# Moving every TensorE operand to a multiple of 128 bytes in an attention and token-mixing layer

## The chip, the cores and the metric

The kernel runs on one core of one Trainium2 chip. The time is the device time of one execution in microseconds, from start to end of the program. Three runs gave 1501.23, 1501.57 and 1502.23 us, median 1501.57 us. The profile is of one more execution.

## The reference

Eight sequences of 1024 tokens with 256 features. Each is normalised over its features, goes through attention with 8 query heads that share one key and one value head of 128 dimensions, and through a gated mix with the token before. Both results are added to the input.

```python
xn = layernorm(x)                                # x: 8 x 1024 x 256, float32
q = xn @ Wq + bq;  k, v = split(xn @ Wkv + bkv)  # q: 8 heads of 128; one k, one v
q, k = q + pe, k + pe                            # sinusoidal positions
p = softmax(causal(q @ k.T / sqrt(128)))         # per head, 1024 x 1024
attn = concat_heads(p @ v) @ Wo
xr, xk = mix of xn and xn one token earlier, with mu_r, mu_k
ffn = sigmoid(xr @ W_r.T) * (relu(xk @ W_k.T) ** 2 @ W_v.T)
out = x + attn + ffn
```

## The kernel before, in words

The precision is kept with pairs. Each operand of a product is split into a high part and a rest (`xt[0]`, `xt[1]`; `wq[0]`, `wq[1]`; and so on), and `product` (L1034) issues three matmuls for each: high by high, high by rest, rest by high. All are of type float32r. In `nc.tensor.matmul(out, a, m)` the first operand `a` is the standing one, loaded into the array by a weight load of 128 columns; `m` is the moving one, which streams past it. The transposes (`pT`, `xn`, `kv`) are of type float32, with the data standing and `ident` moving.

The queries are handled in 64 steps for each sequence (`turns`, L119). A step covers 16 tokens of all 8 heads. `turn` on TensorE (L1131) issues in a fixed order, written out by hand: the transposes of the probabilities of an earlier step (L1143), what the tables `TURNS` and `WO_AT` list for the step (`fill`, L1073: queries Q, keys and values KV, the gated mix FK, FR, FV, the output projection WO), the products of probabilities and values for each second step (L1181, L1190), and the scores of the step (L1211 through L1040). Which operand stands and which moves:

| product | standing | moving | columns |
|---|---|---|---|
| Q, KV, FK | `wq`, `wkv`, `wk` | `xt`, `xt`, `mh` | 256 |
| FR | `mh` | `wr` | 256 |
| FV | `kh` | `wv` | 256 |
| WO | `ot` | `wo` | 256 |
| probabilities by values | `v`, `vn`, `vs` | `pt` | 256 |
| scores | `qt` | `kt` | 16 to 512 |

Scores wider than 512 columns are made in two halves of equal width; the second half starts in `kt` wherever the first ends, a multiple of 32 bytes. VectorE adds the mask to the scores and writes `X` (L1019), ScalarE takes the exponential (L764), GpSimd divides by the sum (L571), and TensorE transposes, or VectorE does (L923) and DMAs carry `Y` to memory and back into `pt` (park L436, fetch L448).

The arrays of on-chip memory are laid out one after the other in the order in which `build` names them (L208 to L250), each rounded up to 32 bytes. The first, `xt`, starts at byte 640 of each partition. As every size up to `wo` is a multiple of 1024, `xt`, `mh`, `wv`, `kt`, `pt` and `wo` all start 128 bytes past a multiple of 256. Behind `wo` stands `gap`, an array of 64 bytes that nothing uses. So `wq`, `wk`, `wkv`, `wr`, `kh`, `qt`, `v`, `vs`, `vn` and `ot` start 192 bytes past a multiple of 256. Small tables then shift what follows: `ident` and `kv` start at 192, `xn` and `X` at 160, `Y` at 224, each past a multiple of 256. Slices that the program takes out of the standing arrays start 512 bytes apart or a multiple of that, and the slices of `pt` 128 bytes apart.

Of the kernel before, what the change touches and what calls it, by code (L numbers as in the profile page):

```python
# [5 lines left out]
H, D = 8, 128  # L6
P = 128
CT = E // P
CHUNK = 256
TPC = CHUNK // P  # L10
NC = T // CHUNK
NT = T // P
# [177 lines left out]
def build(nc, x_d, wq_d, wkv_d, wo_d, wr_d, wk_d, wv_d, bq_d, bkv_d, mu_d, pet_d, out_d, park_d):  # L190
# [6 lines left out]
    with ExitStack() as ctx:  # L197
        def sb(name, shape, dt=F):
            return ctx.enter_context(nc.sbuf_tensor(name, shape, dt))
# [4 lines left out]
        def sem(name):  # L204
# [6 lines left out]
        kt = [sb(f"kt{i}", [P, T], R) for i in range(2)]  # L211
        pt = [sb(f"pt{i}", [P, 2 + i, 2 * NT * P], R) for i in range(2)]
        wo = [sb(f"wo{i}", [P, H, E], R) for i in range(2)]
        gap = sb("gap", [P, 16])
        wq = [sb(f"wq{i}", [P, CT, H * D], R) for i in range(2)]
        wk = [sb(f"wk{i}", [P, CT, E], R) for i in range(2)]
        wkv = [sb(f"wkv{i}", [P, CT, 2 * D], R) for i in range(2)]
# [4 lines left out]
        vs = sb("vs", [P, TPC, D], R)  # L222
        vn = sb("vn", [P, NT, D], R)
        ot = [sb(f"ot{i}", [P, H, P], R) for i in range(2)]
        bq = sb("bq", [P, H])
        mu = sb("mu", [P, 4])
        omu = sb("omu", [P, 4])
        bkv = sb("bkv", [P, 2])
        pet = sb("pet", [P, T])
        mask = sb("mask", [P, WIDE], mybir.dt.bfloat16)  # L230
        gap2 = sb("gap2", [P, 24])
        ident = sb("ident", [P, P])
        xtok = sb("xtok", [P, NC, TPC, E])
        kv = sb("kv", [P, 2, CHUNK])
        stats = sb("stats", [P, TPC, 6])
        mv = sb("mv", [P, TPC, 2])
        rstd = sb("rstd", [P, TPC])
        vare = sb("vare", [P, TPC])
        half = sb("half", [P, TPC])
        xnt = sb("xnt", [P, CT, CHUNK + 1])  # L240
        qtmp = sb("qtmp", [P, QTMP, 2, CHUNK])
        mix = sb("mix", [P, CT, CHUNK])
        ka = sb("ka", [P, CT, CHUNK])
        gate = sb("gate", [P, TPC, E])
        xn = sb("xn", [P, TPC, E])
        X = sb("X", [P, 10, T // 2])
        bias = sb("bias", [P, 10])
        total = sb("total", [P, 10])
        rec = sb("rec", [P, 10])
        Y = sb("Y", [P, 2, 4, NT, 32])  # L250
        steps_of = X[:, 9, 0:P].rearrange("p (h c) -> p h c", h=H)

        pS = [pb(f"pS{i}", [P, 2, 512]) for i in range(2)]
# [82 lines left out]

        STAGE = {"wq0": X[:, 0:CT, :],
                 "wq1": X[:, CT:2 * CT, :],
                 "wkv": X[:, 4, :].rearrange("p (t n) -> p t n", t=CT),
                 "wk": X[:, 5, :].rearrange("p (t n) -> p t n", t=CT),  # L340
                 "wr": X[:, 6:6 + CT, E:2 * E],
                 "wv": X[:, 8:8 + CT, E:2 * E],
                 "wo0": Y[:, 0, :, :, :].rearrange("p a k c -> p a (k c)"),
                 "wo1": Y[:, 1, :, :, :].rearrange("p a k c -> p a (k c)")}
        W = {"wq0": [w[:, :, 0:H * D // 2] for w in wq], "wq1": [w[:, :, H * D // 2:H * D] for w in wq],
# [12 lines left out]
        def x_row(s, lo, hi):  # L358

            j, n = halves_of(s)  # L360
            return X[:, j:j + n, :].rearrange("p h n -> p (h n)")[:, lo:hi]
# [40 lines left out]
        def _(sp):  # L402
# [27 lines left out]
            def park(b, s):  # L430
# [3 lines left out]
                if k >= 4:  # L434
                    sp.wait_ge(landed[k % 4], 64 * (k // 4))
                sp.dma_start(park_d[k % 4, :, :, 0:nk * 32],  # L436
                             Y[:, k % 2, :, 0:nk, :].rearrange("p a k c -> p a (k c)")).then_inc(parked[k % 2], 16)

# [349 lines left out]
        def _(dve):  # L788
# [119 lines left out]
            def turn(b, it):  # L908
# [6 lines left out]
                if s in TURNED:  # L915
# [5 lines left out]
                    if k >= 2:  # L921
                        dve.wait_ge(parked[k % 2], 16 * (k // 2))
                    nc.vector.transpose(Y[:, k % 2, :, 0:nk, :].rearrange("p a k c -> p k a c"),  # L923
                                        x_row(s, 0, nk * P).rearrange("p (k a c) -> p k a c", a=4, c=32)
# [362 lines left out]
```

## Time and profile before

| | us |
|---|---|
| median of three runs | 1501.57 |
| the profiled execution, its own time | 1506.69 |
| its span, first to last instruction | 1504.9 |
| TensorE matmuls busy | 1482.6 |
| weight loads busy (beside the matmuls) | 1448.2 |
| VectorE busy | 1268.4 |
| GpSimd busy | 1128.9 |
| ScalarE busy | 1068.0 |

The mean granted TensorE clock was 0.997 of the full 2.4 GHz. Busy time is the union of what an engine's instructions cover. A matmul's recorded duration runs from its start until its last result, and the next matmul starts long before that, so durations of neighbours overlap; a run of equal matmuls is timed by the distance of the starts of the groups before and after it.

### The profile page before, as it was taken

What the parts mean: (1) busy time and instruction counts of PE and PEld (TensorE: products, weight loads), DVE (VectorE), ACT (ScalarE), POOL (GpSimd) and SP (SyncE); (2) the same over time, 40 slices, a digit from 0 to 9 for tenths busy, and PEclk for the clock granted to TensorE, in tenths of its full rate; (3) what the DMA queues carried; (4) which work ended last, traced back from release to release, by engine and by line L of the source; (5) the groups of instructions that cost most, each with busy time, mean ns of one, the idle gap of its engine ahead of it and who ended that gap; (6) DMA issues with size and microseconds to landing.
All of it is one profiled execution on the core that took longest, in us unless ns stands there. A gap on an engine that the chain in (4) does not pass through costs nothing.

```text
span 1504.9 us, 36254 instructions
## 1 busy us (share of the span) xinstructions
PE 1482.6 (99%) x11724; PEld 1448.2 (96%) x11724; DVE 1268.4 (84%) x3424; ACT 1068.0 (71%) x2563; POOL 1128.9 (75%) x1541
## 2 busy tenths in 40 slices
PE   7999999999999999999999999999999999999998
PEld 7999999999999999999999999999999999999998
DVE  6999878898788987998879888798977888789885
ACT  6777667776677767767677776776767777677764
POOL 6687777777777877777777776777777787777875
PEclk8999999999999999999999999999999999999999
DMA  4144422444224442244423444134441344403453
GB/s 129 48 131 129 142 75 64 134 125 147 72 65 133 135 134 68 83 120 137 134 60 88 127 128 144 46 98 128 134 141 34 113 131 138 136 27 108 119 157 105
DMA packets 225801, 164.39 MB, mean 109 GB/s; under 512 B 51792, under 2 KB 220880, under 8 KB 225616
## 3 DMA queue, kind: packets, MB, share of 16 engines
q1 hardware_dynamic: 224768, 161.69, 35.6%
q8 instruction: 96, 1.57, 0.4%
q14 instruction: 89, 0.73, 0.2%
q10 hardware_dynamic: 848, 0.40, 0.1%
HBM read 81.27 MB, written 77.59 MB: 106 GB/s over the span
## 4 chain that ended last, share of the span: by engine, by line
PE 81%; DVE 10%; issue 4%; POOL 3%; DMA 1%; ACT 1%; SPq 0%; DVEq 0%; POOLq 0%; ACTq 0%
PE pS L1040 27%; PE pO L1181 22%; PE pG L1040 13%; PE pG L1127 9%; PE pT L1143 8%; DVE X L1019 2%; DVE pt L943 1%; DVE Y L923 1%; DVE kt L831 1%; POOL X L571 1%; DVE xn L808 1%; DMA park_dram<-Y 1%; DVE mix L860 1%; POOL qt L527 1%; DVE qtmp L849 1%
## 5 line engine op out<-in xcount | busy, mean ns | idle before, releaser
L764 ACT ACTIVATE X<-X,bias 128x16 f32<-128x16 f32 (+56 forms) x512 | 376.1, 734 | 150.7 <-DVE bias L1019 149.0
L1040 PE MATMUL pS<-kt,qt 128*128 128x288 f32 (+41 forms) x2304 | 460.1, 329 | 4.5 <-DVE bias L1019 3.4
L571 POOL TENSOR_SCALAR X<-X,rec 128x16 f32<-128x16 f32 (+56 forms) x512 | 378.2, 739 | 44.2 <-DVE rec L913 33.4
L1040 PEld LDWEIGHTS pS<-kt,qt 128*128 128x128 f32 x2304 | 365.7, 189 | 17.1 <-issue 5.3
L546 POOL TENSOR_TENSOR pt<-pt 128x256 fp32r<-128x256 f32 (+5 forms) x192 | 316.6, 1649 | 60.3 <-ACT pt L686 59.8
L1181 PE MATMUL pO<-pt,v 128*128 128x256 f32 x2192 | 307.6, 284 | 1.2 <-DVE ot L998 0.9
L1019 DVE CUSTOM_DVE_ANT_1 X<-pS,mask 128x528 f32<-128x528 f32 (+31 forms) x256 | 245.6, 959 | 47.1 <-PE pS L1040 42.3
L1181 PEld LDWEIGHTS pO<-pt,v 128*128 128x128 f32 x2192 | 271.9, 189 | 2.6 <-DVE ot L998 2.1
L943 DVE TENSOR_TENSOR pt<-pt,pT 128x512 fp32r<-128x512 f32 (+3 forms) x440 | 207.6, 493 | 35.1 <-ACT pt L692 32.2
L757 ACT CAST ot<-pO 128x256 fp32r<-128x256 f32 x256 | 95.5, 373 | 184.0 <-PE pO L1181 117.8
L692 ACT CAST pt<-pT 128x512 fp32r<-128x512 f32 (+3 forms) x448 | 188.0, 450 | 30.8 <-PE pT L1143 30.5
L527 POOL TENSOR_TENSOR qt<-qtmp,qt 128x512 fp32r<-128x512 f32 x124 | 162.1, 1310 | 57.5 <-ACT qt L659 57.2
L1127 PE MATMUL pG<-wo,ot 128*128 128x256 f32 x1536 | 194.0, 283 | 2.2 <-ACT ka L739 1.5
L1143 PE MATMUL pT<-ident,X 128*128 128x128 f32 x1248 | 190.3, 274 | 0.9 <-DVE pt L943 0.6
L1127 PEld LDWEIGHTS pG<-wo,ot 128*128 128x128 f32 x1536 | 183.0, 189 | 3.5 <-ACT ka L739 2.8
L923 DVE STREAM_TRANSPOSE Y<-X 128x384 f32<-128x384 f32 (+5 forms) x192 | 172.5, 898 | 10.5 <-POOL X L571 9.4
L1181 PE MATMUL pO<-pt,vn 128*128 128x256 f32 x1096 | 171.1, 281 | 0.0
L686 ACT ACTIVATE pt<-pt 128x384 fp32r<-128x384 f32 (+5 forms) x192 | 150.2, 783 | 19.3 <-DMA pt<-park_dram 17.5
L1143 PEld LDWEIGHTS pT<-ident,X 128*128 128x128 f32 x1248 | 150.6, 141 | 10.4 <-issue 0.8
L998 DVE TENSOR_TENSOR ot<-pO,ot 128x256 fp32r<-128x256 f32 x256 | 107.1, 418 | 51.1 <-ACT ot L757 47.9
L1181 PEld LDWEIGHTS pO<-pt,vn 128*128 128x128 f32 x1096 | 146.6, 188 | 0.0
L569 POOL MEMSET X<- 128x16 f32 (+5 forms) x336 | 47.9, 142 | 130.6 <-DVE rec L913 129.7
(120 smaller groups left out, 2298.6 us busy)
## 6 DMA issues: line engine op xcount, KB each, us to landing
park_dram<-Y SPq DMA_DIRECT2D x32, 512.0 KB, 2.6
pt<-park_dram SPq DMA_DIRECT2D x128, 128.0 KB, 2.8
park_dram<-Y SPq DMA_DIRECT2D x32, 448.0 KB, 3.0
pt<-park_dram SPq DMA_DIRECT2D x128, 112.0 KB, 2.5
park_dram<-Y SPq DMA_DIRECT2D x32, 384.0 KB, 2.9
pt<-park_dram SPq DMA_DIRECT2D x128, 96.0 KB, 2.3
park_dram<-Y SPq DMA_DIRECT2D x32, 320.0 KB, 2.7
pt<-park_dram SPq DMA_DIRECT2D x128, 80.0 KB, 2.1
```

What stands on the lines that cost most here:

```text
L527: nc.gpsimd.tensor_tensor(qt[1][:, slot, :, 2 * p:2 * p + 2, :].rearrange("p t i q -> p i t q"), qtmp[:, p % QTMP, :, :].rearrange("p i (t ...
L546: nc.gpsimd.tensor_tensor(low, low.bitcast(F), high.bitcast(F), ALU.add).then_inc(turned_lo, 1)
L571: nc.gpsimd.tensor_scalar(x_row(s, 0, w), x_row(s, 0, w), rec[:, j:j + 1], sign(s), ALU.mult, ALU.mult).then_inc(normed, 1)
L692: nc.scalar.copy(pt_of(0, b, s)[:, s % 2, :, k:k + nk, :].rearrange("p a k c -> p k a c"), pT[u % 2][:, 0:nk * P].rearrange("p (k a c) -> ...
L764: nc.scalar.activation(x_row(s, 0, w), x_row(s, 0, w), ACT.Exp, bias=bias[:, j:j + 1], scale=-1.0, accum_out=total[:, j:j + 1]).then_inc(e ...
L923: nc.vector.transpose(Y[:, k % 2, :, 0:nk, :].rearrange("p a k c -> p k a c"), x_row(s, 0, nk * P).rearrange("p (k a c) -> p k a c", a=4, ...
L943: last = nc.vector.tensor_tensor(low[:, k:k + whole, :, :], high[:, k:k + whole, :, :].bitcast(F), pT[u % 2][:, 0:whole * P].rearrange("p ...
L1019: nc.vector.tensor_tensor_reduce(out=o, in0=scores, in1=m, scale=SCALE, scalar=HUGE, op0=ALU.add, op1=ALU.min, accum_out=bias[:, j:j + 1]) ...
L1040: last = nc.tensor.matmul(out, a[i], m[j], start=start and k == 0, stop=stop and k == n - 1)
L1127: last = nc.tensor.matmul(out[:, 0:E], ot[i][:, h, :], wo[j][:, h, :], start=(i, j, h) == (0, 0, 0), stop=i == 1 and h == H - 1)
L1143: last = nc.tensor.transpose(pT[u % 2][:, i * P:(i + 1) * P], x_row(s, (k + i) * P, (k + i + 1) * P), ident[:, :])
L1181: last = nc.tensor.matmul(summed, (vn if j else v[i])[:, k, :], pt_of(j, b, part)[:, :, :, k, :], start=n == 0, stop=n == 3 * nk - 1)
```

## The change

Nothing but the order of the arrays changes. `gap` goes, so that the ten arrays behind it move down by 64 bytes and start, like the six before them, 128 bytes past a multiple of 256. The small tables (`bq`, `mu`, `omu`, `bkv`, `stats` and the like) and `xnt` move to the end, behind the large arrays, and `Y` moves ahead of `xnt`. With them gone, `pet`, `mask`, `ident`, `xtok`, `kv`, `qtmp`, `mix`, `ka`, `gate`, `xn`, `X` and `Y` start at a multiple of 128; `ident`, `kv`, `xn`, `X` and `Y` at a multiple of 256. No instruction, wait or DMA is added, removed or moved.

```diff
         wo = [sb(f"wo{i}", [P, H, E], R) for i in range(2)]
-        gap = sb("gap", [P, 16])
         wq = [sb(f"wq{i}", [P, CT, H * D], R) for i in range(2)]
...
         ot = [sb(f"ot{i}", [P, H, P], R) for i in range(2)]
-        bq = sb("bq", [P, H])
-        mu = sb("mu", [P, 4])
-        omu = sb("omu", [P, 4])
-        bkv = sb("bkv", [P, 2])
         pet = sb("pet", [P, T])
...
         kv = sb("kv", [P, 2, CHUNK])
-        stats = sb("stats", [P, TPC, 6])
...
-        xnt = sb("xnt", [P, CT, CHUNK + 1])
         qtmp = sb("qtmp", [P, QTMP, 2, CHUNK])
...
         X = sb("X", [P, 10, T // 2])
+        Y = sb("Y", [P, 2, 4, NT, 32])
+        xnt = sb("xnt", [P, CT, CHUNK + 1])
+        bq = sb("bq", [P, H])
+        mu = sb("mu", [P, 4])
...
         bias = sb("bias", [P, 10])
         total = sb("total", [P, 10])
         rec = sb("rec", [P, 10])
-        Y = sb("Y", [P, 2, 4, NT, 32])
```

## Rows read from the trace of the kernel before

**Rows 1.** The page's busy times: engine, us, share of the span, instructions

```profile
PE 1482.6 (99%) x11724; PEld 1448.2 (96%) x11724; DVE 1268.4 (84%) x3424; ACT 1068.0 (71%) x2563; POOL 1128.9 (75%) x1541
```

**Rows 2.** Busy time by stretch, all engines; columns named in its first line

```profile
core 0: us, PE busy (x) PEld busy (x) DVE busy (x) ACT busy (x) POOL busy (x), PEclk, DMA share, GB/s
0.00:50.00 50.00, 40.32 (x281) 38.24 (x282) 38.18 (x123) 31.70 (x85) 31.51 (x58) 0.90 0.30 98
150.00:700.00 550.00, 545.45 (x4342) 533.55 (x4341) 468.14 (x1264) 393.16 (x949) 415.62 (x567) 1.00 0.36 108
700.00:1400.00 700.00, 697.16 (x5556) 681.99 (x5555) 593.13 (x1623) 503.52 (x1220) 533.41 (x731) 1.00 0.36 107
1460.00:1505.00 45.00, 40.56 (x310) 38.06 (x309) 26.30 (x51) 22.35 (x40) 24.73 (x23) 1.00 0.33 110
```

**Rows 3.** The page's chain that ended last, shares by engine

```profile
PE 81%; DVE 10%; issue 4%; POOL 3%; DMA 1%; ACT 1%; SPq 0%; DVEq 0%; POOLq 0%; ACTq 0%
```

**Rows 4.** Views of single tiles, matmuls: count, duration ns min/median/max, first and last start

```profile
L1040 PE MATMUL pS<-wv,kh x192: 276/276/367, 45.3 to 1374.6; 128*128 128x256 f32 x192
L1040 PE MATMUL pS<-wr,mh x192: 277/279/363, 34.0 to 1351.9; 128*128 128x256 f32 x192
L1040 PE MATMUL pG<-wr,mh x192: 277/279/363, 104.0 to 1462.9; 128*128 128x256 f32 x192
L1040 PE MATMUL pS<-mh,wk x192: 276/281/365, 20.2 to 1343.6; 128*128 128x256 f32 x192
L1040 PE MATMUL pG<-mh,wk x192: 276/276/386, 84.6 to 1428.5; 128*128 128x256 f32 x192
L1040 PE MATMUL pG<-xt,wq x924: 276/281/550, 15.4 to 1419.7; 128*128 128x256 f32 x185
L1040 PE MATMUL pS<-xt,wq x600: 276/276/561, 12.4 to 1370.3; 128*128 128x256 f32 x150
L1127 PE MATMUL pG<-wo,ot x1536: 276/281/391, 51.3 to 1501.9; 128*128 128x256 f32 x192
L1181 PE MATMUL pO<-pt,v x2192: 276/279/388, 35.8 to 1497.3; 128*128 128x256 f32 x200
L1181 PE MATMUL pO<-pt,vn x1096: 276/281/286, 36.2 to 1498.3; 128*128 128x256 f32 x183
```

**Rows 5.** Timeline of TensorE: start us, us, engine, line, operation, count

```profile
674.87 1.30 PE L1181 MATMUL pO<-pt,v 128*128 128x256 f32 x10
676.00 0.74 PE L1181 MATMUL pO<-pt,vn 128*128 128x256 f32 x5
676.58 1.12 PE L1040 MATMUL pS<-kt,qt 128*128 128x352 f32 x6
677.54 1.57 PE L1040 MATMUL pG<-xt,wq 128*128 128x256 f32 x12
...
681.91 1.34 PE L1181 MATMUL pO<-pt,v 128*128 128x256 f32 x10
683.09 0.75 PE L1181 MATMUL pO<-pt,vn 128*128 128x256 f32 x5
```

**Rows 6.** Groups by line and form, 730.21 to 730.23 us, the end of an FR

```profile
L1040 PE MATMUL pG<-wr,mh 128*128 128x256 f32 x3 | 0.5, 278 | 0.0
```

**Rows 7.** Groups by line, 725.95 us (first half) and 726.65 us (second)

```profile
L1040 PE MATMUL pS<-kt,qt 128*128 128x464 f32 x2 | 0.6, 372 | 0.0
L1040 PE MATMUL pS<-kt,qt 128*128 128x464 f32 x2 | 0.6, 374 | 0.0
```

**Rows 8.** Views of the tiles `kv` and `X`, transposes on TensorE

```profile
L1095 PE MATMUL pG<-ident,kv x46: 270/270/271, 80.1 to 1422.7; 128*128 128x128 f32 x46
L1143 PE MATMUL pT<-ident,X x1248: 270/272/457, 31.3 to 1491.2; 128*128 128x128 f32 x179
```

**Rows 9.** From the page's costliest groups and its DMA issues

```profile
L1019 DVE CUSTOM_DVE_ANT_1 X<-pS,mask 128x528 f32<-128x528 f32 (+31 forms) x256 | 245.6, 959 | 47.1 <-PE pS L1040 42.3
park_dram<-Y SPq DMA_DIRECT2D x32, 512.0 KB, 2.6
```

**Rows 10.** Waits, longest in total: engine, line, releaser, us, times, longest

```profile
ACT pt L686 <- DMA pt<-park_dram: 17.5, 25, 2.0
```

More of the change, by code:

```diff
@@ L234, in build @@
         kv = sb("kv", [P, 2, CHUNK])
-        stats = sb("stats", [P, TPC, 6])
[L236 to L239, printed above, removed]
-        xnt = sb("xnt", [P, CT, CHUNK + 1])
         qtmp = sb("qtmp", [P, QTMP, 2, CHUNK])
@@ L246, in build @@
         X = sb("X", [P, 10, T // 2])
+        Y = sb("Y", [P, 2, 4, NT, 32])
+        xnt = sb("xnt", [P, CT, CHUNK + 1])
+        bq = sb("bq", [P, H])
+        mu = sb("mu", [P, 4])
+        omu = sb("omu", [P, 4])
+        bkv = sb("bkv", [P, 2])
+        stats = sb("stats", [P, TPC, 6])
+        mv = sb("mv", [P, TPC, 2])
+        rstd = sb("rstd", [P, TPC])
+        vare = sb("vare", [P, TPC])
+        half = sb("half", [P, TPC])
         bias = sb("bias", [P, 10])
```

## The prediction

> **What bounds the kernel now.** I read the busy times first. TensorE's matmuls cover 99% of the span and the weight loads beside them 96%, VectorE 84% [rows 1]. Busy time overstates a pipelined engine, so the next view is the same by stretch: from 150 to 1400 us TensorE stands idle for 4.6 of 550 us and 2.8 of 700 us, and only the first 50 and the last 45 us hold gaps of 9.7 and 4.4 us [rows 2]. The chain that ended last gives TensorE 81% and VectorE 10% [rows 3]. So what changes the distance between matmul starts changes the time nearly one for one, and the question is whether a matmul's pace depends on where its operands lie.
>
> It does vary. A matmul of 256 columns takes 276 ns at the least, in every kind but FR's; yet the medians stand at 276, 279 and 281 [rows 4]. The timeline turns this into pace. Ten matmuls of probabilities by values take 676.00 - 674.87 = 1.13 us in one place, 113 ns each; the same ten, same arrays, take 683.09 - 681.91 = 1.18 us in another, 118 ns each [rows 5]. A duration of 276 goes with a pace of 113, one of 281 with 118. I counted all distances between starts behind a matmul of 256 columns (rows 5 show five such groups of the whole trace): 3380 are at most 115 ns, 4200 lie from 116 to 129, 395 are longer (a wait, or the first behind transposes). The two paces come in runs: once entered, one is mostly kept through the groups that follow, until transposes come. They don't go with DMA traffic or with what the other engines do at the moment; the same step of every sequence mostly shows the same pace. That looks like TensorE's own two reads getting in each other's way: the moving operand of one matmul and the standing operand of the next, which is loaded beside it.
>
> **Where the addresses show.** Call D the start of the moving operand less the start of the standing one that loads beside it, modulo 256 bytes.
> - Most kinds have moving 128 and standing 192, D = 192: both paces, 276 and 281.
> - FR has them the other way round, `wr` at 192 and `mh` at 128, D = 64: its least is 277 and its median 279, in both banks [rows 4], never the 276 of the rest.
> - `vn` with `pt` is the only kind at 256 columns whose moving start changes in steps of 128: its median is 281 [rows 4]. It reads eight runs of 32 elements. Where they lie an odd multiple of 128 bytes apart, all 192 matmuls that start at D = 64 take 279 or more, but only 43% of the 264 at D = 192. Where they lie an even multiple apart (632 matmuls), 96 to 100% are slow at either distance.
> So D matters at 256 columns, most of all for a moving operand that is read in one piece. After the change it is 0 in all kinds except the half of `vn`'s at D = 128. The trace holds D = 0 for float32r in two places:
> - The last matmul of an FR group: `wr` at 192 moves while `v` or `qt` at 192 loads. There are 32. In 27 it takes 277 ns behind neighbours of 279, in five 281. At one such end the mean over the last three is 278, two of 279 and one of 277 [rows 6]. The group behind it then has D = 192 again.
> - Score matmuls in second halves whose start in `kt` falls on 192. At 464 columns the first half (D = 192) means 372 ns and the second (D = 0) 374 [rows 7]. Over the 64 such distances I find 0.7 ns more on average than in first halves of the same width.
> Both are single passes through D = 0 between other distances, not a long run at it; that is the weak point of what follows.
>
> **The sum, against the profiled execution (1506.69 us; span 1504.9).**
> 1. The 7952 matmuls of 256 columns. At D = 192, 3380 of 7580 undisturbed ones have the short pace, 45%. The ends of FR say 27 of 32, 84%, at D = 0. As these are single ones, I take half the way, 65%, for all but the 632 of `vn` that are slow at any distance: 20% of 6948 is 1390 matmuls, at 4.7 ns (118 - 113, less some for those between): -6.5 us. Bounds: all short is -17.7 us (the sum of what each of the 4200 now has over 113.4, cut at 118); all long is 3380 x 4.9 = +16.4 us.
> 2. FR's 384 are in this count, but start from 279 and not from a mixture: 384 x 2 ns = -0.8 us more if they reach 277. From 0 to -1.1.
> 3. Scores. First halves and undivided scores over 256 columns, 384 + 768 = 1152 matmuls, go from D = 192 to D = 0: 1152 x 1 ns = +1.2 us, from 0 to +2.3 (rows 7 taken for all). The second halves run through all distances in steps of 32 before and after, so what one gains another loses: 0, within 2 us.
> 4. The 1440 transposes. `kv` by `ident` has D = 0 now (both 192) and takes 270 ns, `X` by `ident` has D = 32 and takes 272 [rows 8]; after it both are D = 0. No gain is counted; at most 1248 x 2 ns = -2.5 us, and no loss, as a row at D = 0 stands there.
> 5. VectorE, ScalarE, GpSimd. `X` moves from 160 to 0, `qtmp`, `mix`, `ka`, `gate` likewise. No instruction of the trace does the same work at two starts, so there is no row for it. If the mask step at 959 ns [rows 9] lost or gained 1% in each of 256, that is 2.5 us, of which 10 to 20% would reach the path [rows 3]: 0, within 1 us.
> 6. DMAs out of `Y` (224 to 0) and `xtok` (192 to 0). A park lands in 2.6 us [rows 9], and the whole wait of ScalarE for what comes back is 17.5 us [rows 10], on an engine busy for 71%. A tenth of the landing either way is hidden by the tables, which let a step or more (1505 us by 512 steps is 2.9 us) pass between fetch and use: 0. Were that cover gone, 10% of 17.5 is 1.8 us.
> The steps make -6.5 - 0.8 + 1.2 = -6.1 us of TensorE's time. Some of it turns into waits for VectorE, which works at 84%: I pass on nine tenths, -5.5 us. That would be 1501.2 us for the profiled execution. It ran 5.1 us above the median of the three, so I take the difference to the median: 1501.57 - 5.5 = 1496.1 us.
>
> The Trainium skill speaks against any effect: "TensorE: Matmul & The Clock Gate", section "Step-by-step: what each phase is for", gives the engine two independent read ports, so that "Loading the next tile's weights doesn't steal SBUF read bandwidth from the running matmul". By that rule term 1 is nothing and the time stays at 1501.6. This trace does not agree as it stands: equal matmuls take 276 and 281 ns [rows 4] with nothing else in step with them.
>
> **Rivals.**
> - *Long runs at D = 0 lock into the slow pace.* FR at D = 64 does so in each group, and `vn`'s D = 64 half nearly so [rows 4]; D = 192 may be the one lucky distance, and 0 as bad as 64. Against it: the 27 of 32 ends of FR, and that the pace behind an FR end is set anew. It decides when the share of 281s passes the present 55%. All long: +16.4 + 1.2 = 17.6, nine tenths is 15.8: 1517 us. Two thirds of the short ones lost: 1512.
> - *Nothing changes* (scores at D = 0 and 192, 0.7 ns apart, speak for it). Which pace a run takes may hang on the phase in which it is entered and not on D; then the shares are dealt anew and come out alike. Time 1501.6, within 3 us.
> - *The gain is whole*: D = 0 holds nearly all at the short pace: -17.7 - 0.8 - 2.5 + 1.2 = -19.8, nine tenths -17.8: 1484 us.
> - *Another engine pays.* A new start makes VectorE's steps on `X` longer; from 2% (19 ns of 959) on half of the score steps would wait longer, since VectorE is 84% busy: 256 x 19 ns on the path, +4.9 us: with no gain elsewhere, 1506.
>
> **How the numbers follow.** Partial gain 0.35 (1489 to 1499), whole gain 0.12, no change 0.20, slow pace 0.27, another engine 0.06. I name the partial gain's value, 1496.1. Its own range is 1489 to 1499. The range that leaves out 2 in 10 runs from 1485, close to the whole gain, to 1514, inside the slow pace. A measurement of this kernel tells 0.2%, 3 us, from no change. Faster by more 0.47, same 0.20, slower by more 0.33.
>
> **What would show it.** Right if in the tile views `wr,mh` shows 276 or 277 as its median, the medians of `wo,ot` and `pG<-xt,wq` fall from 281 to 276, and a count of the distances gives about two thirds at 115 ns or less, with TensorE's busy time down by 6 us. Wrong if those medians stand at 281 everywhere (slow pace), or if shares move but come out alike. Term 3 is wrong if score durations of the same width differ by more than 2 ns between the profiles, term 4 if transposes leave 270 to 272, term 5 if mean durations on VectorE, ScalarE or GpSimd move by over 1%. If the time moves by more than 3 us while TensorE's durations don't, the whole reading falls.

## The result: slower by 1.2%, and the profile after

| | before | after |
|---|---|---|
| median, four runs each, us | 1501.90 | 1521.61 |
| lowest to highest, us | 1501.23 to 1502.84 | 1520.84 to 1523.01 |
| the profiled execution, us | 1506.69 | 1523.01 |
| its span, us | 1504.9 | 1520.6 |

The ratio on record is 1.0124 (95% interval 1.0111 to 1.0136); that of the two medians is 1.0131, 19.7 us. I forecast 1496.1 with a range of 1485 to 1514: wrong in sign, and the range missed. In a later measurement, on chip 4 (that of the first isn't on record), the changed kernel gave 1.0162 [1.0143, 1.0181].

First the changed kernel's busy times and the shares of its chain, to be read beside [rows 1, 3]:

```profile
PE 1504.5 (99%) x11724; PEld 1473.6 (97%) x11724; DVE 1258.1 (83%) x3424; ACT 1069.7 (70%) x2563; POOL 1134.8 (75%) x1541
PE 92%; DVE 3%; POOL 1%; DMA 1%; issue 1%; SPq 1%; ACT 1%; DVEq 0%; ACTq 0%; POOLq 0%
```

TensorE gained 21.9 us of busy time and 11 points of the chain. The loads beside its matmuls gained 25.4 us. GpSimd and ScalarE stand within 6 us of before, and VectorE got 10 us shorter. By stretch (columns as in [rows 2]):

```profile
core 0: us, PE busy (x) PEld busy (x) DVE busy (x) ACT busy (x) POOL busy (x), PEclk, DMA share, GB/s
150.00:700.00 550.00, 549.22 (x4306) 538.67 (x4305) 459.00 (x1252) 389.55 (x939) 414.37 (x564) 1.00 0.35 107
700.00:1400.00 700.00, 700.00 (x5489) 686.80 (x5488) 580.11 (x1606) 496.62 (x1201) 530.03 (x717) 1.00 0.35 106
```

The loss is even over the length: 4306 matmuls in 550 us where there were 4342, 5489 in 700 us where there were 5556. The 4.6 and 2.8 us in which TensorE stood idle have shrunk to 0.8 and 0. The granted clock is 1.00 in both. So each matmul takes longer, and it is the same everywhere. The views of the tiles, against [rows 4, 8], say which:

```profile
L1039 PE MATMUL pS<-wv,kh x192: 280/283/365, 45.5 to 1389.8; 128*128 128x256 f32 x192
L1039 PE MATMUL pS<-wr,mh x192: 278/283/364, 34.2 to 1366.6; 128*128 128x256 f32 x192
L1039 PE MATMUL pG<-mh,wk x192: 274/282/283, 85.5 to 1442.8; 128*128 128x256 f32 x192
L1039 PE MATMUL pG<-xt,wq x924: 276/283/550, 14.7 to 1433.9; 128*128 128x256 f32 x185
L1126 PE MATMUL pG<-wo,ot x1536: 277/283/384, 51.5 to 1517.5; 128*128 128x256 f32 x192
L1180 PE MATMUL pO<-pt,v x2192: 277/283/387, 36.1 to 1512.9; 128*128 128x256 f32 x200
L1180 PE MATMUL pO<-pt,vn x1096: 279/282/288, 36.4 to 1513.9; 128*128 128x256 f32 x183
L1094 PE MATMUL pG<-ident,kv x46: 270/270/274, 81.0 to 1436.9; 128*128 128x128 f32 x46
L1142 PE MATMUL pT<-ident,X x1248: 270/272/458, 31.0 to 1506.6; 128*128 128x128 f32 x179
```

Every median at 256 columns is 282 or 283. Not only is 276 gone; 283 is longer than the 281 of the longer pace before. The transposes stand where they stood. The timeline of TensorE, for the same ten products of probabilities by values as in [rows 5]:

```profile
680.96 1.36 PE L1180 MATMUL pO<-pt,v 128*128 128x256 f32 x10
682.16 0.76 PE L1180 MATMUL pO<-pt,vn 128*128 128x256 f32 x5
...
688.12 1.36 PE L1180 MATMUL pO<-pt,v 128*128 128x256 f32 x10
689.32 0.76 PE L1180 MATMUL pO<-pt,vn 128*128 128x256 f32 x5
```

682.16 - 680.96 = 1.20 us for ten in both places: 120 ns each, where before one place had 113 and the other 118.

Where the 15.7 us of the span are, by my sums over the distances between TensorE's starts in the two whole traces:

| TensorE's starts, us | before | after | |
|---|---|---|---|
| 256 columns, distances under 130 ns: count, mean | 7580, 116.01 ns | 7587, 119.56 ns | 7587 x 3.55 ns = +26.9 |
| of these at most 115 ns | 3380 | 93 | |
| 256 columns, longer ones, what they have over 118 ns | 42.1 | 38.0 | -4.1 |
| behind scores, all | 393.5 | 388.8 | -4.7 |
| behind transposes, all | 141.3 | 138.7 | -2.6 |

26.9 - 4.1 - 4.7 - 2.6 = 15.5. The pace costs 27 us. 11 us of that are won back in waits. A slower TensorE waits less for VectorE and ScalarE, but part of the 11 us is chance: the profiled execution of the kernel before took 5.1 us more than its median, the changed kernel's only 1.4. By the medians the loss is 19.7 us, so some 7 us come back, if the pace is the same in executions without a profile.

### The profile page after: what moved, and what is told of

Same layout as the page of the kernel before. It is cut to its first block, busy times and chain, and to the rows that moved or that the text cites. A ratio compares the mean times of both kernels' runs of the same rounds, so it can differ in the third digit from the quotient of the medians.

```text
span 1520.6 us, 36254 instructions
## 1 busy us (share of the span) xinstructions
PE 1504.5 (99%) x11724; PEld 1473.6 (97%) x11724; DVE 1258.1 (83%) x3424; ACT 1069.7 (70%) x2563; POOL 1134.8 (75%) x1541
## 4 chain that ended last, share of the span: by engine, by line
PE 92%; DVE 3%; POOL 1%; DMA 1%; issue 1%; SPq 1%; ACT 1%; DVEq 0%; ACTq 0%; POOLq 0%
PE pS L1039 31%; PE pO L1180 25%; PE pG L1039 14%; PE pG L1126 11%; PE pT L1142 8%; DMA park_dram<-Y 1%; DVE X L1018 1%; PE pG L1084 0%; PE pO L1189 0%; PE pS L1084 0%; DVE qtmp L848 0%; SPq L447 0%; POOL X L570 0%; PE pG L1094 0%; DVE xn L807 0%
## 5 line engine op out<-in xcount | busy, mean ns | idle before, releaser
L1180 PE MATMUL pO<-pt,v 128*128 128x256 f32 x2192 | 316.0, 288 | 1.1 <-DVE ot L997 0.9
L1180 PEld LDWEIGHTS pO<-pt,v 128*128 128x128 f32 x2192 | 279.4, 191 | 2.3 <-DVE ot L997 2.0
L1126 PE MATMUL pG<-wo,ot 128*128 128x256 f32 x1536 | 199.3, 286 | 1.1 <-ACT ot L756 0.6
L1126 PEld LDWEIGHTS pG<-wo,ot 128*128 128x128 f32 x1536 | 188.1, 192 | 1.5 <-ACT ka L738 0.7
```

The source lines that it names most:

```text
L1126: last = nc.tensor.matmul(out[:, 0:E], ot[i][:, h, :], wo[j][:, h, :], start=(i, j, h) == (0, 0, 0), stop=i == 1 and h == H - 1)
L1180: last = nc.tensor.matmul(summed, (vn if j else v[i])[:, k, :], pt_of(j, b, part)[:, :, :, k, :], start=n == 0, stop=n == 3 * nk - 1)
```

## The experiments

The theory after the result: what counts is D, the moving start less the standing start modulo 256 bytes, and in a long run D = 0 has a pace of its own, 120 ns. Rivals: the tables and large arrays that also moved, or the moving or the standing start by itself. A ratio is to the kernel before, measured together with it on the same chip, with its 95% interval; the medians are of 4 to 12 executions, those of the kernel before of 7 to 23. A distance between starts of at most 115 ns is called short. D is given in bytes.

### 1. Only the distance: `gap` behind `ot`

```diff
         wo = [sb(f"wo{i}", [P, H, E], R) for i in range(2)]
-        gap = sb("gap", [P, 16])
...
         ot = [sb(f"ot{i}", [P, H, P], R) for i in range(2)]
+        gap = sb("gap", [P, 16])
```

The ten arrays from `wq` to `ot` move down by 64 bytes; everything behind them stays.

> The layout of before, but the 64 unused bytes stand behind ot instead of behind wo. So the ten arrays from wq to ot start 128 past a multiple of 256, as in the changed kernel, and everything else starts where it did. Theory A, the loss comes from the distance D between what moves and what stands (192 before, 0 now): this kernel is as slow as the changed one, 1519 to 1523 us, and its matmuls of 256 columns have medians of 282 to 283 ns. Theory B, the loss comes from the moved X, Y, ident and small tables: it stays at 1501 to 1503 us, with medians of 276 to 281.

Measured: 1530.68 against 1504.77 us, 1.0174 [1.0159, 1.0189]. The tile `ot` of this kernel:

```profile
L1127 PE MATMUL pG<-wo,ot x1536: 277/283/387, 51.7 to 1523.2; 128*128 128x256 f32 x192
```

The median is 283, the mean distance 119.50 ns, 89 are short: the whole loss, by the place of these ten arrays alone. The time lies above the 1519 to 1523 us expected, though the pace is that of the changed kernel (119.56); part 8 comes back to this.

### 2. Only the rest: tables and large arrays moved, D kept

In the changed kernel:

```diff
         wo = [sb(f"wo{i}", [P, H, E], R) for i in range(2)]
+        gap = sb("gap", [P, 16])
...
         ot = [sb(f"ot{i}", [P, H, P], R) for i in range(2)]
+        gap1 = sb("gap1", [P, 16])
```

> The changed kernel with the 64 unused bytes put back behind wo and 64 more behind ot: wq to ot start at 192 past a multiple of 256 as before, the small tables stand at the end, and the large arrays behind ot start at multiples of 128. Theory A: 1500 to 1504 us, medians 276 to 281. Theory B: 1519 to 1523 us.

The large arrays stand at multiples of 128 here, but `ident`, `kv`, `xn`, `X` and `Y` at 128 past a multiple of 256, where the changed kernel has them at 0.

Measured: 1502.51 us, 0.9986 [0.9976, 0.9996]: nothing, or a seventh of a per cent gained. The tile `ot`:

```profile
L1128 PE MATMUL pG<-wo,ot x1536: 276/281/387, 50.3 to 1496.8; 128*128 128x256 f32 x192
```

The distances average 116.25 ns, close to the 116.01 of before. The rival of the moved tables falls.

### 3. The distance by itself: a series on TensorE

A kernel that leaves out the whole layer: VectorE fills arrays at eight standing starts and three moving starts, and TensorE then runs groups of matmuls, with four transposes between groups, while no other engine works.

```python
for m in (128, 0, 192):                 # moving start
    for s in range(0, 256, 32):         # standing start
        turns(4)                        # transposes
        mm(m, s, 0, 30)                 # 30 matmuls of 256 columns
```

> No attention here: a series of matmuls of type float32r on arrays with chosen starts, with no other engine at work beside TensorE, the input copied to the output. Groups of 30 matmuls of 256 columns, each with its own weight load, moving start 128, 0 or 192 and standing start 0, 32, ... 224 past a multiple of 256 (arrays sta to sth), four transposes ahead of each group; then the same behind two matmuls of 300 columns, groups of 512 columns, and moving operands read in eight runs. Theory A, what counts is the distance D of moving less standing: the eight paces come back for each moving start, shifted; at D = 0 119 to 120 ns, at D = 64 117 to 118, at D = 192 113 or 118. Theory A2, only the standing start counts: equal paces for equal standing letters, the slowest at 128 (ste) and the quickest at 192 (stg). Theory C, the paces come from the other engines' accesses to the same memory: all groups alike near 113 ns here.

Four groups on the timeline, each with the transposes behind it: D = 0 and D = 192 with the moving start at 128, then D = 0 and 192 with it at 0.

```profile
62.80 3.83 PE L73 MATMUL pO<-movhalf,ste 128*128 128x256 f32 x30
66.47 0.60 PE L68 MATMUL pT<-ident,xs 128*128 128x128 f32 x4
...
70.81 3.68 PE L73 MATMUL pO<-movhalf,stg 128*128 128x256 f32 x30
74.33 0.60 PE L68 MATMUL pT<-ident,xs 128*128 128x128 f32 x4
...
78.64 3.85 PE L73 MATMUL pO<-movzero,sta 128*128 128x256 f32 x30
82.33 0.60 PE L68 MATMUL pT<-ident,xs 128*128 128x128 f32 x4
...
86.67 3.67 PE L73 MATMUL pO<-movzero,stc 128*128 128x256 f32 x30
90.17 0.60 PE L68 MATMUL pT<-ident,xs 128*128 128x128 f32 x4
```

3.67 and 3.69 us at D = 0, 3.52 and 3.50 at D = 192: some 0.17 us, 6 ns a matmul, at both moving starts. The distance behind each group's first matmul is about 200 ns and the next few are unsettled, so I take the mean from the ninth on:

| D | 0 | 32 | 64 | 96 | 128 | 160 | 192 | 224 |
|---|---|---|---|---|---|---|---|---|
| moving at 128 | 119.9 | 116.7 | 117.8 | 120.1 | 118.5 | 117.4 | 113.3 | 118.5 |
| moving at 0 | 120.0 | 116.5 | 117.8 | 120.1 | 118.8 | 117.2 | 113.3 | 118.4 |
| moving at 192 | 120.0 | 116.7 | 117.8 | 120.1 | 118.8 | 117.4 | 117.8 | 118.4 |

Three moving starts give one curve in D, but for D = 192, which has two paces. So it is neither start by itself, no third engine is needed, and 113.3, the least seen, belongs to D = 192, which is where the kernel before had put nearly all. D = 0 is next to the slowest. The first distances at D = 0 were 116, 119, 116 ns: only a longer run settles at 120. It does so each time: eight groups at D = 0 with 128 standing columns, in three series and behind different entries, settle at 119.9 to 120.3. At 512 columns D = 0 is the shortest instead (226.7 ns, 228.9 at D = 64, 233.3 to 233.9 at the other six).

With the moving operand in eight pieces of 32, as `vn` with `pt`, the order changes: 384 bytes apart (odd multiple of 128) D = 192 has 113.3, 0 has 120.0; 256 bytes apart (even) D = 192 has 120.0 and 0 has 117.8. That agrees with the split of `vn`'s counts in the prediction.

### 4. Another distance: D = 64, and FR as its mirror

In the kernel before:

```diff
-        gap = sb("gap", [P, 16])
+        gap = sb("gap", [P, 48])
```

All kinds go to D = 64 (`vn` with `pt` to 64 and 192, as `pt` starts in steps of 128), but FR, whose moving operand is in the moved group, goes to D = 192.

> The kernel of before with 192 unused bytes behind wo instead of 64: wq to ot start 64 past a multiple of 256, so D is 64 where it was 192; for FR alone it becomes 192 (wr moves from 192 to 64). The sweep on its own arrays gives 117.8 ns at D = 64, 113.3 or 117.8 at 192 and 120.0 at 0. If the pace depends on D alone: mean distance of the undisturbed 256-column matmuls 117.8 ns where before has 116.0 and the changed kernel 119.6; time 13 us over before, 1515 us (ratio 1.008 to 1.010), and FR is now the one kind with 276s. If what counts is that 0 is special: as before, 1502 to 1505 us.

Measured: 1511.82 against 1504.79 us, 1.0041 [1.0026, 1.0057]. The tiles `ot` and `wr`:

```profile
L1127 PE MATMUL pG<-wo,ot x1536: 276/279/387, 50.9 to 1506.8; 128*128 128x256 f32 x192
...
L1040 PE MATMUL pG<-wr,mh x192: 276/276/369, 106.4 to 1467.5; 128*128 128x256 f32 x192
```

The two have changed places: `wo,ot` now has the median of 279 that FR had in [rows 4], and FR in bank `pG` has 276. FR's short share, of its undisturbed distances, rises from 0.08 to 0.43, and it is the only kind whose mean pace falls clearly (117.6 to 116.0). All of that is bank `pG` (0.85 short): FR in bank `pS` has D = 192 too and not one short distance, 117.9 ns. So D = 192 allows the short pace and doesn't bring it. The sign is right and the size is half of what I expected: the mean is 117.28 and not 117.8, since 0.28 of `wo,ot` and 0.18 of `pt,v` stayed short. The series has no short pace at D = 64, so it doesn't carry over whole.

### 5. Only the scores at D = 0

In the kernel before, `qt` ahead of `gap`:

```diff
         wo = [sb(f"wo{i}", [P, H, E], R) for i in range(2)]
+        qt = [sb(f"qt{i}", [P, 2, CHUNK // SUB, H, SUB], R) for i in range(2)]
         gap = sb("gap", [P, 16])
...
-        qt = [sb(f"qt{i}", [P, 2, CHUNK // SUB, H, SUB], R) for i in range(2)]
```

> The kernel of before with qt ahead of the 64 unused bytes: only the scores (kt moves, qt stands) get D = 0 in place of 192, all other products keep theirs. If the loss of the changed kernel lies in the matmuls of 256 columns alone, this stays at before within 3 us (1502 to 1506). The sweep shows 226.7 ns at D = 0 against 233.3 at 192 for 512 columns in long runs: if that holds for the groups of three of this kernel, scores over 256 columns (1152 in first halves and undivided ones) gain up to 6.6 ns each, 0 to 7 us. If scores carry part of the loss, it is 5 us or more slower.

Measured: 1501.97 us, 0.9982 [0.9971, 0.9992]. The sum of the distances behind scores is 393.0 us, 393.5 before: the scores themselves gained nothing. What moved is the matmuls of 256 columns behind them, whose D is the same as before: 4025 short ones instead of 3380, mean 115.68 instead of 116.01, 2.5 us. The tile `ot`:

```profile
L1127 PE MATMUL pG<-wo,ot x1536: 276/276/387, 50.8 to 1496.3; 128*128 128x256 f32 x192
```

281 has become 276 with no change to where `wo` and `ot` lie; `mh,wk` in bank `pG` went the other way, from 0.87 short to 0.04. That looks like the pace that is set on entry, seen in the kernel. It isn't fully shown: `wq` to `kh` have moved up by 32 KB, and there is only one trace of the kernel before, so how far its 3380 vary from execution to execution isn't known.

### 6. What the distance costs, and what sets the pace on entry: a second series

Again the layer is left out. (a) standing starts in steps down to 4 bytes; (b) fewer standing columns; (c) three matmuls of another width ahead of each group at D = 192; (d) other widths.

```python
for cols in (32, 64, 96, 128):                                  # (b)
    for s in (128, 192, 64): turns(4); narrow(s, cols, 18)
for entry in (264, 280, 288, 304, 320, 344, 384, 416, 448, 512):  # (c)
    turns(4); mm(0, 192, 0, 3, entry); mm(128, 192, 0, 18)
```

> A second series of matmuls with nothing beside TensorE. (a) Standing start moved from 192 by single elements, -12 to +12 elements of 4 bytes. Theory bank: two reads that meet in the same part of memory hold each other up, and what counts is the distance in steps of the line, so paces change in steps of 16 or 32 bytes. (b) Standing operand of 32, 64, 96 and 128 columns at D = 0, 192 and 64: if the weight load's read is what collides, D stops to matter as the load gets shorter, at 32 columns all are within 1 ns of 109 to 110; if D acts without the load, 120 stays. (c) Eighteen matmuls at D = 192 entered behind three of 264 to 512 columns: if the phase of the entry picks the pace, some entries give 113 and others 118, and each keeps it to the end. (d) Widths from 64 to 480 columns at eight distances: under 256 columns the weight load bounds, 107 to 115 ns whatever the width; over it the excess over columns / 2.4 falls at D = 0 as it does at 512.

Part (a) was placed wrongly by me, around D = 64 instead of 192. It has 116.7 ns at D = 48, 117.9 at 60, 117.7 at 64, 117.5 at 68, 118.4 at 72, 120.0 at 112. No step of 16 or 32 bytes stands out. The 0.2 ns between neighbours 4 bytes apart are less than what the entry alone makes at one D (116.7 or 120.0 at D = 32, part 9), so whether single elements matter isn't shown.

Part (b), D = 0 with 32 and with 128 standing columns, and (c), D = 192 behind three matmuls of 344 and of 384 columns:

```profile
83.27 2.29 PE L89 MATMUL pO<-movhalf,ste 128*32 128x256 f32 x18
85.40 0.60 PE L68 MATMUL pT<-ident,xs 128*128 128x128 f32 x4
...
106.04 2.40 PE L89 MATMUL pO<-movhalf,ste 128*128 128x256 f32 x18
108.28 0.60 PE L68 MATMUL pT<-ident,xs 128*128 128x128 f32 x4
...
128.88 2.28 PE L73 MATMUL pO<-movhalf,stg 128*128 128x256 f32 x18
130.99 0.60 PE L68 MATMUL pT<-ident,xs 128*128 128x128 f32 x4
...
131.95 2.21 PE L73 MATMUL pO<-movhalf,stg 128*128 128x256 f32 x18
134.00 0.60 PE L68 MATMUL pT<-ident,xs 128*128 128x128 f32 x4
```

(b): 2.13 us against 2.24, 6 ns a matmul. The settled pace at D = 0 is 113.3, 113.9, 115.4 and 120.0 ns for 32, 64, 96 and 128 standing columns. The moving operand is the same in all four: what D = 0 costs goes with how much is loaded beside it. A narrower standing operand also makes a narrower result, 32 partitions of `pO` instead of 128, and nothing here keeps the two apart. At D = 64 the width matters by 1 ns only (116.7 to 117.8), and at D = 192 it isn't monotonic (113.3, 119.0, 117.2, 113.3). The 109 to 110 ns that I had expected at 32 columns were seen at no distance (113.3, 113.3, 116.8).

(c): 2.11 against 2.05 us for the same 18 matmuls. Behind 264, 280, 320, 384, 416 and 448 columns the pace settles at 113.3, behind 288, 304, 344 and 512 at 117.8, and each stays to the end of the group. D = 192 has two stable paces, and what went before picks one. It isn't the width alone: behind three matmuls of 288 columns the third series has 113.3 at D = 192, with two transposes ahead instead of four and the standing slices taken in threes instead of fours.

(d) contradicts the expectation for the widths between: by the mean of the fourth to eleventh distances D = 0 isn't the shortest at 416 columns (188.9 ns, 186.6 at D = 192) nor at 448 (202.6, 199.9 at D = 64). So the gain at 512 columns can't be carried over to the scores, which gained nothing in part 5.

### 7. Distances chosen

In the changed kernel: `gap` back, `qt` ahead of it, and `wr` behind `ot` and 128 bytes of tables, so that it starts at 64 and FR too has D = 192.

```diff
         wo = [sb(f"wo{i}", [P, H, E], R) for i in range(2)]
+        qt = [sb(f"qt{i}", [P, 2, CHUNK // SUB, H, SUB], R) for i in range(2)]
+        gap = sb("gap", [P, 16])
...
-        wr = [sb(f"wr{i}", [P, CT, E], R) for i in range(2)]
...
+        bq = sb("bq", [P, H])
+        mu = sb("mu", [P, 4])
+        omu = sb("omu", [P, 4])
+        bkv = sb("bkv", [P, 2])
+        wr = [sb(f"wr{i}", [P, CT, E], R) for i in range(2)]
```

> A version meant to beat both: the order of the changed kernel, but wq, wk, wkv, kh, v, vs, vn and ot at 192 (D = 192), wr at 64 so that FR has D = 192 as well, qt at 128 (scores D = 0), everything behind ot at 128 or 0 as in the changed kernel. Against before: FR's 384 matmuls go from 117.6 to about 115.5 ns (-0.8 us), scores 0 to -7 us, the moved tables and X 0 to -3 us. Expected 1499 us, 1494 to 1503, beside a before of 1502 to 1505. If D did not matter, this would be the changed kernel's time.

Measured: 1500.19 against 1504.79 us, 0.9969 [0.9959, 0.9979], ahead of both kernels. It is the lowest ratio of all, but its interval overlaps those of parts 2, 5 and 9, so it isn't shown to be the fastest. The tile `wr` in bank `pG`, where [rows 4] has 279:

```profile
L1040 PE MATMUL pG<-wr,mh x192: 276/276/369, 104.0 to 1455.9; 128*128 128x256 f32 x192
```

FR's pace falls from 117.6 to 115.0 ns, 1 us over its 384. But the mean over all is 116.29, no better than before: the other kinds lost what FR won. In this trace the gain over the kernel before stands in fewer waits (behind scores 390.3 us instead of 393.5, behind FK 48.0 instead of 51.1). The trace of the kernel before, with its 5.1 us over the median, overstates that, and why there are fewer I can't say.

### 8. The changed kernel again, and its other halves of the layout

Parts 1 and 2 give 1.0174 and 0.9986, and the changed kernel itself 1.0124. To see whether half a per cent is due to the tables, one chip ran the changed kernel again, the same with the small tables at their old places in the order, and with the large arrays off their multiples of 128:

```diff
--- tables in place
...
+        gap4 = sb("gap4", [P, 16])
+        xnt = sb("xnt", [P, CT, CHUNK + 1])
+        gap5 = sb("gap5", [P, 24])
...
--- large arrays off
+        gap1 = sb("gap1", [P, 16])
...
+        gap4 = sb("gap4", [P, 24])
```

> The changed kernel itself, beside the next two on one chip: 1.011 to 1.014 of before.

> The changed kernel, but the small tables and xnt stand where they stood before, with unused bytes that keep the large arrays behind ot at multiples of 128 (X and xn at 0, ident and kv at 128 past a multiple of 256). The one-part run with only wq to ot moved was at 1.0174 of before, the changed kernel at 1.0124. Theory T, the half per cent comes from the place of the tables (scalars that VectorE, ScalarE and GpSimd read): 1.016 to 1.019. Theory L, it comes from the starts of the large arrays: 1.011 to 1.014. Theory N, neither: the waits of the hand-written schedule fall differently for any layout: anything from 1.010 to 1.019.

> The changed kernel with the tables at the end, but pet at 192, ident and kv at 64 and xn, X and Y at 160 past a multiple of 256. Theory T: 1.011 to 1.014. Theory L: 1.016 to 1.019. Theory N: anything between.

Measured: 1.0162 [1.0143, 1.0181], 1.0159 [1.014, 1.0179], 1.0150 [1.0134, 1.0166]. The three agree, so tables and large arrays count for nothing that can be told. The changed kernel doesn't agree with itself, 1.0124 there and 1.0162 here (1.011 to 1.014 was expected). TensorE's waits of the two traces (releaser, us in all, times, longest), first the first run's:

```profile
PE pG L1126 <- ACT ka L738: 0.5, 1, 0.5
...
PE pS L1039 <- DVE bias L1018: 0.2, 1, 0.2
```

and those of the later one:

```profile
PE pS L1039 <- DVE bias L1018: 3.7, 8, 0.9
PE pG L1126 <- ACT ka L738: 3.4, 7, 0.5
```

The pace is the same to the hundredth (119.56 ns, 93 and 95 short ones). 6.4 us of the 8.6 by which the spans differ (1520.6 and 1529.2) stand in these two waits. So the 27 us of pace are the fixed part; how much comes back as shorter waits was 11 us in one trace and 2.6 in the other, both against the one trace of the kernel before.

### 9. A third series, and D = 168 in the kernel

D in steps of 8 bytes, 18 matmuls each, entered from two transposes, or with three matmuls of 288 or 344 columns between.

> A third series with nothing beside TensorE: 18 matmuls of 256 columns at each D from 0 to 248 in steps of 8 bytes, entered in three ways (two transposes; the same and three matmuls of 288 columns; or of 344). If D = 192 is a single lucky distance: 117 to 120 ns at nearly all others in all three entries, 113 or 118 at 192. If short paces form a band around 192, some distance in it, 176 to 208, gives 113 in all three entries, and a layout with it would make the kernel faster by up to 4500 x 4.7 ns = 21 us.

D = 168 and D = 176, entered from transposes:

```profile
96.51 2.34 PE L87 MATMUL pO<-movhalf,stg 128*128 128x256 f32 x18
98.69 0.38 PE L68 MATMUL pT<-ident,xs 128*128 128x128 f32 x2
98.83 2.38 PE L87 MATMUL pO<-movhalf,stg 128*128 128x256 f32 x18
101.05 0.38 PE L68 MATMUL pT<-ident,xs 128*128 128x128 f32 x2
```

2.18 against 2.22 us. D = 168 settles at 113.3 from all three entries, the only one of 32 that does. D = 192 has 117.8, 113.3, 117.8; D = 88 has 120, 113.3, 119.9; D = 32 has 120.0, 116.7, 116.8; D = 0 has 120.0, 120.0, 120.3. So the kernel was given D = 168 throughout, with the standing arrays cut from one that starts so that they lie at 216 and `wr` at 40:

```diff
-        wq = [sb(f"wq{i}", [P, CT, H * D], R) for i in range(2)]
...
+        stood = sb("stood", [P, 22 + 12544 + 20 + 1024], R)
+        wq = [part(CT, H * D) for i in range(2)]
...
+        taken[0] += 20
+        wr = [part(CT, E) for i in range(2)]
```

> The chosen layout of the fifth run with D = 168 where it had 192: wq, wk, wkv, kh, v, vs, vn and ot stand 216 past a multiple of 256 (cut out of one array, so that a start need not be a multiple of 32) and wr at 40, so that FR has 168 too; 480 of vn's matmuls get D = 40. qt keeps D = 0. The series by 8 bytes gave 113.3 ns at 168 from all three entries, 113 or 118 at 192, 120 at 0 and at 40. If the paces of the series carry over to this kernel, whose standing slices go on in other orders and whose runs are short: about nine tenths of the 6900 matmuls outside vn at 113 to 115 ns, mean of the undisturbed ones 114 to 114.5 against 116.3 of the chosen layout and 116.0 of before, time 1486 to 1492 us beside a before of 1504 (ratio 0.988 to 0.992; nine tenths of 7590 x 1.9 ns is 13 us on top of the 0.3% it had). If 168 was an accident of the series' slices: 1500 us or more.

Measured: 1500.82 against 1504.1 us, 0.9976 [0.9966, 0.9986]. The expectation missed. The tiles:

```profile
L1136 PE MATMUL pG<-wo,stood x1536: 276/276/513, 52.1 to 1501.2; 128*128 128x256 f32 x192
L1049 PE MATMUL pG<-stood,mh x192: 282/282/367, 105.9 to 1462.3; 128*128 128x256 f32 x192
```

`wo` has the median of 276, with 0.58 of its undisturbed distances short (0.39 before). FR got 282 at the same distance, none to speak of short, 120.0 ns. All in all 3446 are short, mean 116.09: what it was. The series took slices of its arrays in another order than the kernel does, and FR's differ from `wo`'s. It also needed five to eight matmuls at D = 168 before it reached 113 ns, and an FR group has 12. I did not test which of that matters.

## Why the prediction was wrong

**Step 1 is the one that failed, and by its evidence.** It took the share of the short pace at D = 0 as 65%, half way to the 27 of 32 at the ends of FR [rows 6]. It came out at 93 of 7587, 1%. I had named the weak point myself: single passes. The series shows why it is weak. The first matmuls at D = 0 show 116 and 119 ns, and only in a longer run do all have 120; one matmul's duration tells of the state that it was entered in, not of its own distance. Of the 27 us, 15.1 are 7587 x (118 - 116.01), all going to the slow pace that was seen, and 11.8 are 7587 x (119.56 - 118): a slower one that the trace didn't show in a long run, though it was there in part: 289 of `vn`'s 1094 undisturbed matmuls took 282 or 283 ns, 119.5 ns apart. The ends of FR themselves, 115 ns apart in 27 of 32 before, are 120 ns apart in all 32 after, now that they stand in a long run at D = 0. Predicted -6.5 us, and at worst +16.4; measured +26.9. The sum had a slip besides: 45% is the short share of all 7580, and of the 6948 without `vn`'s slow ones it is 49%, so that 65% would have been -5.4 us; and 3380 x 4.9 is 16.6.

The rival that long runs lock into the slow pace was the right mechanism. At 1512 to 1517 us it was too small by that third level, even after 11 us came back in waits. The trace could have given it more weight than 0.27: each long run at another distance than 192 was slow ([rows 4]; within FR's groups none of 320 distances is short), against one kind of single passes. Runs should have counted for more. What I took from it, that the pace behind an FR end is set anew, was true and spoke for nothing.

**Step 2** had the sign wrong with step 1: FR went from 279 to 283, from 117.6 to 119.4 ns, not to 277.

**Step 3 is too small to be told.** Distances behind scores, less the waits over 300 ns, went from 382.4 to 383.3 us: +0.9 where +1.2 was forecast. But the same sum is 381.8 in both kernels of parts 1 and 5, where the scores have D = 0 too, and 384.4 in the changed kernel of part 8. Mean durations are 328.7 and 328.3 ns.

**Steps 4 and 6 were right.** Transposes kept 270 and 272, and a park lands in 2.7 us instead of 2.6 (`Y` stood at 96 past a multiple of 256 before, not at 224).

**Step 5** was right in what it gave the layout, but its own sign of being wrong came up: mean durations that move by over 1%. The mask step has 961 ns instead of 959, while VectorE's busy time fell by 10 us; four kinds of step, those that write `mix`, `xn`, `xtok` from `gate`, and `kt`, lost 13 us between them. The last, in the kernel before, the changed one, and the changed one again (part 8):

```profile
L831 DVE SCALAR_TENSOR_TENSOR kt<-kv,kt 128x256 fp32r<-128x256 f32 x32 | 27.1, 848 | 5.3 <-ACT kt L645 5.3
...
L830 DVE SCALAR_TENSOR_TENSOR kt<-kv,kt 128x256 fp32r<-128x256 f32 x32 | 22.6, 706 | 6.0 <-ACT kt L644 6.0
...
L830 DVE SCALAR_TENSOR_TENSOR kt<-kv,kt 128x256 fp32r<-128x256 f32 x32 | 29.6, 926 | 6.0 <-ACT kt L644 6.0
```

848, 706 and 926 ns: as one layout has both 706 and 926, the starts aren't the cause. A VectorE that had less to do in the first trace of the changed kernel fits its shorter waits; that the one caused the other isn't shown. Part 2 puts tables and large arrays together at 0.9986.

**Nine tenths passed through** was a fair value but no constant. Of 26.9 us, 15.7 reached the span in one trace (0.58) and 24.3 in the other (0.90), both against a trace of the kernel before that ran 5.1 us over its median. By the medians it is 19.7 us (0.73) and 25.9 us (0.96). How much VectorE's and ScalarE's lateness leaves to win back differs from run to run.

The reading ahead of the steps held: matmuls' starts set the time, nothing else in the trace goes with the pace, and D matters most for an operand read in one piece. The rule cited there from the Trainium skill ("TensorE: Matmul & The Clock Gate", section "Step-by-step: what each phase is for"), by which loading the next weights takes nothing from the running matmul, isn't what these runs show at 256 float32r columns: the pace depends on where both operands start, and at D = 0 the same moving operand takes 113.3 ns beside a load of 32 columns and 120.0 beside one of 128. The measurement decides; whether it is read bandwidth that is shared isn't shown.

**Open.** What collides inside the chip was not measured, only that it depends on D and goes with the width of what is loaded. Why FR at D = 168 takes 120.0 ns where the series has 113.3 is open, and so is why waits differ between two runs of one kernel.

## What to carry to other kernels

Where TensorE is the bound and each matmul loads its own weights, the start of the moving operand against that of the standing one, modulo 256 bytes, is worth up to 6% of the pace at 256 float32r columns, and giving all operands one alignment (D = 0) was nearly the worst choice. Judge such a distance by long runs of it, never by single matmuls between others. A short series ranks the distances roughly, but its best one must be tried in the kernel itself: it got the sign right for D = 0 and 64, and nothing of the gain it promised for 168.

## What the runs showed of the hardware that I had not expected

- One and the same distance has two stable paces, 113.3 and 117.8 ns at D = 192, chosen by what ran ahead. In the kernel 645 more matmuls had the short pace when only the scores' distance was changed (part 5). Other distances change with the entry too (D = 32, 88), but D = 0 never did.
- In part (d) of the second series TensorE fell to half its clock while it was busy without a gap. The same view by stretch, at 256 columns and with matmuls of 64 and 128 columns, each with its load:

```profile
core 0: us, PE busy (x) PEld busy (x) DVE busy (x) POOL busy (x), PEclk, DMA share, GB/s
113.00:141.00 28.00, 28.00 (x236) 27.92 (x235) 0.00 (x0) 0.00 (x0) 1.00 0.00 1
148.50:187.00 38.50, 38.50 (x188) 38.50 (x188) 0.00 (x0) 0.00 (x0) 0.50 0.00 0
188.50:230.00 41.50, 41.50 (x323) 41.44 (x322) 0.00 (x0) 0.00 (x0) 0.99 0.01 1
```

  The granted clock is 0.50, the 1.2 GHz level, from 148.5 to 187 us, and 0.99, the 2.4 GHz level, from 188.5 to 230 us. Ahead of the fall stood the groups of 256 columns, three groups of 64 columns, one matmul each 111.7 ns, and the start of a fourth. At half clock one takes 213 ns, with 64, 128 or 192 columns. Ahead of the rise stood the first group of 192 columns.
